# Perceiver layer on one core: VectorE's value sum ahead of the lower halves, context splits in three pieces a step sooner

## The reference, cut to what matters

```python
x = x + xattn(layernorm(x), ctx_2048, Wq, Wk, Wv, Wo)     # x: 128 x 512, ctx: 12544 x 512, 16 heads of 128
x = x + attn(layernorm(x), ...)                           # a small linear attention
x = x + ffn(layernorm(x), w1, b1, ln_g, ln_b, w2, b2)     # weights rounded to -1, 0, 1
# xattn: softmax over 12544 context rows
scores = einsum('bqhd,bkhd->bhqk', q, k); attn = softmax(scores); out = einsum('bhqk,bkhd->bqhd', attn, v) @ Wo
```

## Time and profile before

| | |
|---|---|
| median of 3 runs | 2175.51 us (2173.81 to 2178.58) |
| the profiled execution, its own time | 2175.8 us |
| span of the profile | 2173.9 us |
| granted TensorE clock, mean | 0.981 of full speed |
| PE busy | 1984.7 us, 91% (17330 instructions) |
| PEld busy | 1594.6 us, 73% |
| DVE busy | 1660.5 us, 76% |
| ACT busy | 1137.6 us, 52% |
| POOL busy | 294.5 us, 14% |

### The profile page before, as it was taken

How to read it: one execution, slowest core, us unless ns; L and a number is a source line. 1 busy time by engine, 2 the same in 40 slices (tenths; PEclk the granted TensorE clock), 3 DMA queues, 4 the chain that set the end, 5 groups by cost and what they waited for, 6 DMA issues and landing times.

```text
span 2173.9 us, 46145 instructions
## 1 busy us (share of the span) xinstructions
PE 1984.7 (91%) x17330; PEld 1594.6 (73%) x17334; DVE 1660.5 (76%) x3346; ACT 1137.6 (52%) x2484; POOL 294.5 (14%) x465
## 2 busy tenths in 40 slices
PE   5789999999999999999999999999999999999786
PEld 4676886876877877877877877877868868777562
DVE  5777787787878788787888787887888787877426
ACT  3555555565655555555555554555555555545312
POOL 1011111211211111111111121111111111200001
PEclk8899999999999999999999999999999999999988
DMA  5567786887877778777787787786876776765650
GB/s 148 133 118 148 152 158 138 155 150 144 160 133 147 130 134 161 135 147 145 130 148 152 128 157 137 132 160 136 146 150 132 138 136 119 141 119 95 212 193 5
DMA packets 966943, 304.43 MB, mean 140 GB/s; under 512 B 893984, under 2 KB 952864, under 8 KB 965824
## 3 DMA queue, kind: packets, MB, share of 16 engines
q1 hardware_dynamic: 966720, 301.47, 70.9%
HBM read 72.16 MB, written 4.46 MB: 35 GB/s over the span
## 4 chain that ended last, share of the span: by engine, by line
PE 63%; DVE 19%; issue 8%; ACT 6%; DMA 2%; ACTq 1%; SPq 0%; POOL 0%; DVEq 0%; POOLq 0%
PE ps_s L1176 23%; PE ps_t L1176 18%; PE ps_w L1191 11%; PE ps_v L1191 7%; DVE bulk L817 4%; ACT pp L631 4%; DVE prob L863 4%; DVE pp L868 3%; DVE ps_w L887 2%; DVE mx L833 1%; DMA bulk<-in_vo 1%; PE ps_w L1150 1%; ACT alpha L676 1%; PE ps_v L1163 1%; PE ps_t L1270 1%
## 5 line engine op out<-in xcount | busy, mean ns | idle before, releaser
L1176 PE MATMUL ps_s<-bulk 128*128 128x128 f16 (+2 forms) x4752 | 589.0, 274 | 2.9 <-DVE bulk L809 2.7
L1191 PE MATMUL ps_v<-nring,pt 128*128 128x256 f16 x4704 | 581.3, 273 | 3.3 <-DVE acc L877 1.5
L1191 PE MATMUL ps_w<-nring,pt 128*128 128x256 f16 x3528 | 456.2, 274 | 119.4 <-DVE ps_w L887 117.6
L868 DVE SCALAR_TENSOR_TENSOR pp<-prob,pp 128x384 f16<-128x384 f32 (+4 forms) x680 | 515.3, 806 | 62.8 <-ACT pp L631 62.7
L1191 PEld LDWEIGHTS ps_v<-nring,pt 128*128 128x128 f16 x4704 | 458.7, 98 | 64.0 <-DVE acc L792 2.9
L1176 PEld LDWEIGHTS ps_s<-bulk 128*128 128x128 f16 x4752 | 408.4, 99 | 117.3 <-DVE bulk L809 2.9
L1191 PEld LDWEIGHTS ps_w<-nring,pt 128*128 128x128 f16 x3528 | 333.9, 98 | 198.1 <-DVE ps_w L887 155.3
L1176 PE MATMUL ps_t<-bulk 128*128 128x384 f16 (+2 forms) x3564 | 453.5, 272 | 13.9 <-ACT ps_t L651 13.4
L1176 PEld LDWEIGHTS ps_t<-bulk 128*128 128x128 f16 x3564 | 302.2, 98 | 105.0 <-ACT ps_t L651 14.6
L631 ACT ACTIVATE pp<-prob 128x384 f16<-128x384 f32 (+4 forms) x680 | 373.2, 621 | 10.8 <-DVE prob L863 9.7
L863 DVE TENSOR_TENSOR prob<-prob 128x384 f32<-128x384 f32 (+2 forms) x544 | 276.0, 540 | 49.8 <-ACT prob L620 44.7
(11 more groups left out here) (187 smaller groups left out, 1379.0 us busy)
## 6 DMA issues: line engine op xcount, KB each, us to landing
stage<-in_ctx SPq DMA_DIRECT2D x196, 128.0 KB, 2.9
wst<-in_w SPq DMA_DIRECT2D x64, 256.0 KB, 3.2
bulk<-in_vo SPq DMA_DIRECT2D x16, 512.0 KB, 6.0
acc<-in_qk SPq DMA_DIRECT2D x11, 512.0 KB, 3.9
pt<-pp SPq DMA_TRANSPOSE x272, 5.6
tern_d<-wter SPq DMA_DIRECT2D x32, 128.0 KB, 3.0
bulk<-tern_d SPq DMA_DIRECT2D x2, 2048.0 KB, 11.1
nring<-in_aw SPq DMA_DIRECT2D x3, 1024.0 KB, 8.0
```

What stands on the lines that cost most here:

```text
L868: nc.vector.scalar_tensor_tensor(pp_part(k, 1, blk, n), prob_part(k, blk, n), P_SCALE, pp_part(k, 0, blk, n), ALU.mult, ALU.subtract).then ...
L1176: ins = mm(out if n == 1 else out.rearrange("p (n m) -> p n m", m=P), q_part(e, qlo, a)[:, c * P:(c + 1) * P], t_moving(k, run, tlo, b, c) ...
L1191: ins = mm(dst, pt[:, tile:tile + P], n_part(c, clo, b), start=(first and n == 0 and plo == 0 and clo == 0), stop=(last and n == w - 1 and ...
```

## The change

On DVE, value_sum_d moves from behind the first lower half (of 1152 columns) to ahead of it. The 1792 columns of a context split's lower half are cut into pieces of 768, 512 and 512 columns: the first stands at the very start of the step, ahead of the first maximum, the second behind the first probability sum, the third behind the fourth. The three quantizing instructions are cut apart likewise: behind the first probability sum, behind the fourth, and at the step's end. On ACT, split_hi moves from the middle of step SPLIT_AT to the end of the step before, and alpha moves from ahead of the hi_parts to behind them. On POOL, sum_t runs in the step before SPLIT_AT, and waits for s2_done (PE's fourth score product) of that step. On SP, load_ctx is issued one step sooner, as the last thing of its round. ctx_lo now counts three per block.

```diff
@@ SP
+                sp.wait_ge(ctx_lo, 3 * c)
...
-                for c in range(2, NCH):
-                    if SPLIT_AT[c] == k + 1:
-                        load_ctx(c)
                 for c in range(1, NCH):
                     if SPLIT_AT[c] == k - 2:
                         turn_n(c)
...
                     store_w((k - QUANT_AT - 1) // 2)
+                for c in range(2, NCH):
+                    if SPLIT_AT[c] == k + 2:
+                        load_ctx(c)
@@ POOL
-            def sum_t(j):
+            def sum_t(j, at=None):
 
                 pool.wait_ge(in_ctx, 64 * (j + 1))
+                if at is not None:
+                    pool.wait_ge(s2_done, at + 1)
...
-                found = prep_at(k)
-                if found is not None:
-                    sum_t(found)
+                found = prep_at(k + 1)
                 if k:
                     sums(k - 1)
+                if found is not None:
+                    sum_t(found, k)
@@ ACT, step(k)
                 if ii < NP:
                     q_copy(ii)
-                split_hi(k)
...
                 hi_part(k, S4, 1, 4)
+                if visit(k):
+                    for g, h in enumerate(heads_of(k)):
+                        last = nc.scalar.activation(alpha[:, h:h + 1], nmax_of(k, g, 1), ACT.Exp, bias=nmax_of(k, g), scale=-1.0)
+                    last.then_inc(al_done, 1)
                 if ii < NP:
                     q_hi_part(ii)
+                split_hi(k + 1)
@@ DVE
+            PIECES = ((0, 3), (3, 2), (5, 2))
+
+            def split_lo(k, n):
+
                 c = prep_at(k)
                 if c is None:
                     return
+                at, m = PIECES[n][0] * BLK, PIECES[n][1] * BLK
                 v.wait_ge(ctx_hi, c + 1)
...
+                nc.vector.scalar_tensor_tensor(t_part(c, 1)[:, at:at + m], stage[:, at:at + m], CTX_SCALE,
+                                               t_part(c, 0)[:, at:at + m], ALU.mult, ALU.subtract).then_inc(ctx_lo, 1)
@@ DVE, step(k)
             def step(k):
+                if k:
+                    split_lo(k, 0)
                 v.wait_ge(s2_done, k + 1)
...
-                split_lo(k)
...
-                if 0 <= k - QUANT_AT < 4 * WP and (k - QUANT_AT) % 2 == 0:
-                    quant((k - QUANT_AT) // 2)
-                prob_sums(k)
-                lo_part(k, V22, 3, 1)
+                prob_sum(k, 0)
+                split_lo(k, 1)
+                quant(k, 0)
+                for n in range(1, 4):
+                    prob_sum(k, n)
+                split_lo(k, 2)
+                quant(k, 1)
                 if k >= LAG:
                     value_sum_d(k - LAG)
+                lo_part(k, V22, 3, 1)
...
                 add_values(k - LAG, 1)
                 add_values(k - LAG, 0)
+                quant(k, 2)
@@ PE, step(k)
-                pe.wait_ge(ctx_lo, a + w)
+                pe.wait_ge(ctx_lo, 3 * (a + w))
```

More of the change, by code:

```diff
@@ L423, in load_ctx @@
                 if c:
-                    sp.wait_ge(ctx_lo, c)
+                    sp.wait_ge(ctx_lo, 3 * c)
                 for n, blk in enumerate((B11, B12, B21, B22)):
@@ L429, in turn_n @@
             def turn_n(c):
-                sp.wait_ge(ctx_lo, c + 1)
+                sp.wait_ge(ctx_lo, 3 * (c + 1))
                 if c >= RING:
@@ L673, in step @@
                     value_e_u(k - LAG)
[L674 to L677, removed]
                 hi_part(k, V22, 3, 0)
@@ L810, in q_lo_part @@
                                         ALU.subtract).then_inc(q_lo, 1)
-            def split_lo(k):
+            PIECES = ((0, 3), (3, 2), (5, 2))
+            def split_lo(k, n):
                 c = prep_at(k)
@@ L847, in nm_head, with prob_sum @@
                     nc.vector.tensor_scalar(nmax_of(k, g), whole, -EXP_SCALE, None, ALU.mult).then_inc(nm_done[g], 1)
[L849 to L863, removed]
+            def prob_sum(k, n):
+                dst, a, b, op = ((S1, V21, V22, ALU.add), (S3, V21, V11, ALU.subtract),
+                                 (S2, S1, V11, ALU.subtract), (S4, S2, V12, ALU.subtract))[n]
+                if n == 0:
+                    v.wait_ge(exp_done[0], k + 1)
+                    if k:
+                        v.wait_ge(lo_done, 5 * k)
+                    else:
+                        v.wait_ge(q_lo, 2)
+                if n == 1:
+                    v.wait_ge(exp_done[1], k + 1)
+                if n >= 2:
+                    v.wait_ge(p_sum, 4 * k + n - 1 + (n == 3))
+                nc.vector.tensor_tensor(prob_part(k, dst), prob_part(k, a), prob_part(k, b), op).then_inc(p_sum, 1)
             def lo_part(k, blk, n, place):
@@ L892, in value_sum_e, with quant @@
                 nc.vector.tensor_tensor(val_e, part_v[:, :], val_e, ALU.subtract).then_inc(ve_done, 1)
-            def quant(n):
+            def quant(k, m):
+                if not 0 <= k - QUANT_AT < 4 * WP or (k - QUANT_AT) % 2:
+                    return
+                n = (k - QUANT_AT) // 2
                 piece = wst[:, (n % 2) * D:(n % 2 + 1) * D]
[L896 to L904, removed]
+                if m == 0:
+                    v.wait_ge(in_w[n % 2], 16 * (WP + n // 2 + 1))
+                    nc.vector.tensor_scalar(piece, piece, wsc[:, 4 + n // WP:5 + n // WP], MAGIC, ALU.mult, ALU.add).then_inc(w_step, 1)
+                elif m == 1:
+                    v.wait_ge(w_step, 2 * n + 1)
+                    nc.vector.tensor_scalar(piece, piece, -MAGIC, 1.0, ALU.add, ALU.min).then_inc(w_step, 1)
+                else:
+                    v.wait_ge(w_step, 2 * n + 2)
+                    if n >= 2:
+                        v.wait_ge(out_w[n % 2], 16 * (n // 2))
+                    nc.vector.tensor_scalar(wter[:, (n % 2) * D:(n % 2 + 1) * D], piece, -1.0, None, ALU.max).then_inc(w_quant, 1)
             def step(k):
+                if k:
+                    split_lo(k, 0)
                 v.wait_ge(s2_done, k + 1)
@@ L948, in step @@
                 add_values(k - LAG, 0)
+                quant(k, 2)
             q_out(0)
             q_four_sums(0)
-            split_lo(-1)
+            for n in range(3):
+                split_lo(-1, n)
             q_out(1)
```

2 lines of the change are left out of this document (removed).

## The result

The changed kernel takes **2038.97 us** (median of 4 runs, 2037.31 to 2044.65). The kernel before, run beside it, takes 2174.66 us (2171.35 to 2178.58). Run again in a later group of kernels it gave 2040.34 us and 0.938 [0.936, 0.9399]. The profiled execution took 2039.78 us with a span of 2037.9 us at a mean clock of 0.984.

A forecast was written before the change was run, and what follows sets the result against it. TensorE bounds the kernel, waiting in each step for VectorE's value sum. Off 134.7 + 6 + 4.8 = 145.5 us, on 16: from a span of 2173.9 to 2044.4, so 2046 us; own range 2034 to 2062, whole range 2024 to 2076.

The forecast's parts named there:

- The term of 134.7 us: Steps 7 to 129: the whole PEld wait for the value sum goes, 137.2 us less 0.02 in each of 123 steps.
- 13.62-us step: Sign to look for: steps of 13.62 us where 14.56 stood.
- The clock's 4.8 us: Three falls of PE's clock after 2.4-us stills disappear, 1.6 us each; bounds 0 and 4.8.
- The outside steps' 6 us: A third of 18.1 us of value-sum waits in 13 steps outside 7 to 129 goes; bounds 12 gained to 3 lost.
- The prices of 16 us: Costs set against the gain: 1 us value sum late, 2.4 VectorE's seam, 4.5 ACT's seam, 8 GpSimd's hold of nmax.
- GpSimd's hold of the first nmax (8 us): GpSimd's fourth sum holds nmax, the copy comes 0.43 us later and PE waits 0.18 us in 45 steps; bounds 0, 0.35 each.
- ACT's seam (4.5 us): ScalarE's split at the step's end makes the next copy 0.1 us late for PE in 45 splits; bounds 0, 0.3 each.
- VectorE's (2.4 us): The last quantizing instruction ahead of the split's first piece costs 0.15 us, 16 times; bound 0.5 each, 8 us.
- The value sum late in eight steps (1 us): Where split and quantizing pieces meet, the value sum is 0.1 to 0.4 us late, less its 0.2 margin; 1 us in all.
- the margins' case: Rival, chance 0.18: the value sum's 0.2 us isn't there or VectorE's tail delays PE; 25 us in 124 steps, 2071 us.
- Slack of the tail: VectorE's work behind the moved sum has 0.7 us to spare before it delays the next sum that PE waits for.
- No price at the seams: Rival, chance 0.15: POOL starts late enough or the hold misses PE, ACT's seam has 0.1 more slack; 16 us less, 2030.

The follow-up runs named there:

- first experiment: The kernel before with only the value sum moved ahead of the lower half of 1152 columns: 2082.13 us, ratio 0.9564 to the kernel before.
- third experiment: The changed kernel with the value sum back behind the lower half and alpha back ahead of the hi_parts: 2147.77 us, ratio 0.9869 to the kernel before.
- second experiment: The changed kernel with only the value sum put back behind the lower half of 1152 columns: 2106.6 us, ratio 0.9673 to the kernel before.
- doses: The changed kernel with one memset of 128 columns, four of 44 or eleven of 16 just ahead of the value sum: 2042.09, 2045.17, 2047.87 us.
- fifth experiment: The changed kernel with GpSimd's sums released by PE's second score product (s5_done) in place of the fourth (s2_done): 2037.46 us, ratio 0.9369.
- fourth experiment: The changed kernel with GpSimd's sums no longer waiting for s2_done: 2040.98 us, ratio 0.9377 to the kernel before.
- experiment 11: The kernel before with the value sum moved, and the context load and GpSimd's sums (behind s2_done) a step sooner: 2048.33 us, ratio 0.9413.

## Why the prediction was right, and where its terms were off

**What bounded the kernel** was right: the wait for the value sum, set by VectorE's order. The first experiment moves that one statement and takes 94 us off, and putting it back in the changed kernel costs some 65 us (steps 7 to 130: 1771.40 against 1706.13).

**The term of 134.7 us was too large.** The step that failed is "it costs PE at 2.4 GHz about 0.94 us in each step". Each wait costs the step 0.10 us less than PEld's row shows, and not 0.02. PEld idle by 0.96 us makes 0.86 us of step (14.56 against 13.70, before and third experiment), idle by 0.59 makes 0.49 (second). The trace of before held this: the last product's loads start at 1007.51 with 0.96 us of idle before them, but weight loads run ahead of the matmuls, which were still under way when PEld's idle time began at 1006.55 (1005.69 + 1.15 = 1006.84, in the rows with the doses above). In the second experiment's timeline PE's own row has 0.32 us of idle where PEld's has 0.59. After a wait the first weight load and the first matmul start together, as at 977.88 in the second experiment. In a stream without waits the matmuls follow their loads by 0.11 us: 944.62 for the loads of the product after v7 and 944.73 for its matmuls. That lead is what a wait gives back. So the wait was worth 137.2 - 123 x 0.10 = 124.9 us. The forecast of a 13.62-us step missed by the same 0.08 (13.70).

**The clock's 4.8 us** came: three falls in the kernel before, none between 90 and 1889 us after. The experiments don't isolate it. In the first three PE still stood some 1.1 us in the eight steps, and the granted clock was 1.00 from 126 us at the latest to the end of step 130. So shortening the 2.4-us stills was enough, in one trace of each kernel.

**The outside steps' 6 us** came as 6.6: 3.5 at the start, 0.9 in step 130, whose wait the forecast counted here, and 2.2 in the tail. The third that I took was a choice between bounds, and its closeness is luck.

**The prices of 16 us came to about 1.** This is the other mis-sized sum, and each of its parts was seen:
- GpSimd's hold of the first nmax (8 us). The mechanism was right, and its sizes near: 0.47 us of hold against the forecast's 0.43, and 0.12 us of wait against 0.18:

```profile
950.93 3.15 POOL L546 TENSOR_TENSOR stage<-stage 128x256 f32<-128x256 f32 x4 [3.32 <-PE ps_s L1196]
...
953.47 0.63 DVE L850 SCALAR_TENSOR_TENSOR nmax<-mx,nmax 128x1 f32<-128x1 f32 x1
...
954.13 0.90 ACT L622 ACTIVATE prob<-ps_s,nmax 128x768 f32<-128x768 f32 x1 [3.82 <-DVE nmax L850]
...
955.02 0.37 ACT L639 ACTIVATE ps_w<-ps_v 128x256 f32<-128x256 f32 x1
...
955.51 0.56 PEld L1211 LDWEIGHTS ps_w<-nring,pt 128*128 128x128 f16 x6
```

The sum ends at 954.08, the nmax at 954.10 after 0.63 us in place of 0.16, and the copy ends at 955.39. PE's loads come 0.12 us after their turn (953.36 + 2.01 + 0.02 = 955.39). But a wait of 0.12 us is nearly all absorbed by the same 0.10: a pair of a sum step and a split step takes 27.45 us where two ordinary ones take 27.40. And it shows only where the window doesn't wrap: in the steps that wrap, with twice the instructions, a pair takes 27.62 us with the sums and 27.62 without. That leaves 22 pairs, 22 x 0.05 = 1.1 us, and the fifth experiment, without the hold, is 1.04 us shorter in steps 7 to 130.
- ACT's seam (4.5 us), and VectorE's (2.4 us), on the timeline of the end of step 66:

```profile
960.08 1.69 ACT L611 ACTIVATE bulk<-stage 128x1792 f16<-128x1792 f32 x1
...
961.66 0.47 ACT L653 ACTIVATE ps_t<-ps_s 128x384 f32<-128x384 f32 x1
...
962.32 1.03 PEld L1196 LDWEIGHTS ps_t<-bulk 128*128 128x128 f16 x12
...
963.29 0.74 DVE L884 SCALAR_TENSOR_TENSOR acc<-acc,alpha,ps_w 128x512 f32<-128x512 f32 x1
...
963.95 0.42 DVE L917 TENSOR_SCALAR wter<-wst 128x512 bf16<-128x512 f32 x1
964.28 0.95 DVE L823 SCALAR_TENSOR_TENSOR bulk<-stage,bulk 128x768 f16<-128x768 f32 x1
...
965.15 0.55 DVE L839 TENSOR_REDUCE mx<-ps_s 128x1 f32<-128x384 f32 x1
...
965.62 0.55 DVE L834 CUSTOM_DVE_ANT_0 ps_t<-ps_t,part_e 128x384 f32<-128x384 f32 x1
...
966.28 0.26 PEld L1196 LDWEIGHTS ps_t<-bulk 128*128 128x128 f16 x3
```

The copy ends at 962.13, and PE's loads for ps_t start at 962.32 in their turn. I had it 0.1 us late for two reasons. Each ACT instruction starts some 0.1 us before the one ahead of it ends (960.08 + 1.69 = 961.77, the copy at 961.66), 0.3 us over the chain, and I took off 0.2. And the step is 13.70 us and not 13.62, so PE wants the copy 0.08 us later. VectorE's quantizing piece and the first piece of the split overlap in the same manner. PE's loads that wait for L834 start at 966.28, in their turn: 0.99 us after those before them (965.29), as 964.30 to 965.29. What is left is the eight waits of 0.2 us for L834 in the waits after.
- The value sum late in eight steps (1 us): PEld shows no such wait, and step 64 takes 13.66 us.

**The sum by measured terms**, for steps 7 to 130: 124.9 + 0.9 (step 130) + 4.8 - 1 = 129.6 us against 130.2. Some 0.6 us stay unexplained. The 9.8 us counted too much for the wait and the 15 us counted too much for the prices nearly cancel, and that is luck: the 7 us by which the median is below the forecast are smaller than either error. The range's upper end, 2076, is named for the margins' case, which the forecast's own sum puts at 2071. The time came near neither.

**The margins.** The 0.2 us of the value sum measured 0.19. Behind it lies the 0.1 that a wait gives back, so the rival that had these margins gone (0.18) was 0.3 us a step away. Slack of the tail was 0.7 us by my count. The first experiment shows more: 2.1 us late at step 66 became 0.88 us of wait (0.9 on average, 40.5 / 45), so 1.2 us was slack.

**The rivals.** "No price at the seams", given 0.15, is what happened to the prices (about 1 us of 16), while its time of 2030 us fell with the over-counted wait. The hi_parts never waited for the DMA transposes: ACT shows no wait for a DMA between 136 and 1842 us. What the time did not need was the wait for s2_done (fourth experiment).

**Where the time is now.** PE is busy throughout steps 7 to 130, so hardly a wait is left to take from them. The other 332 us are the start (136) and the tail (196).

## What to carry to other kernels

Look in the waiting engine's partner for the instruction that stands between its release and its result. One statement's place in VectorE's program was worth 94 us here, and the place of one in ACT's program (alpha) 41 us as long as the sum stood behind the lower half. With the sum ahead of it and alpha in its old place (experiment 11), PEld waits in the eight steps alone. When a stall goes, recount what it hid: GpSimd's sums over VectorE's lower halves caused no wait beside a PE that stood still, and cost 34 us beside one that didn't. In this kernel a wait of TensorE was worth what PEld shows less a tenth of a microsecond, and one of a tenth or less next to nothing: look for the same lead of the weight loads before pricing a wait elsewhere.

## What the runs showed of the hardware

- A VectorE instruction of one column with two SBUF inputs was held 0.47 us, to the end of GpSimd's sum (0.63 in place of 0.16 us), while the 384-column sum ahead of it, with one operand in PSUM, took its usual 0.63. Without the overlap the longest of 246 was 163 ns (fifth experiment). The Trainium skill, page "SBUF — State Buffer", section "SBUF: two separate sides", says that such an instruction and a GpSimd operation exclude each other for their whole length; the trace agrees, down to one column.
- Both sides lose when they meet: in the first experiment's step 66 five lower halves took 5.34 us in place of 3.23 and the four sums 4.87 in place of 3.15. Over the whole kernel a sum took 1005 ns on average before (197.0 us in 196) and 727 ns after.
- PE stood still for 2.4 us in eight steps of the kernel before and its clock fell in three of them; at eight stills of 1.1 us (first experiment) it fell in none.
- Short VectorE instructions in a row overlap. Four memsets of 44 columns put the sum off by 0.21 us and eleven of 16 columns by 0.26, some 0.02 to 0.05 us for each further one.
